# Four 1024 KB transfers per batch cut into pieces of 256 KB, and a new order of work on every engine

## The chip, the cores and the metric

The kernel runs on one core of a Trainium2 chip. The metric is the device time of one execution in microseconds; the smaller the better. Before the change the median of three runs is 2786.49 us.

## What is computed

Eight independent batches of 1024 rows by 256 columns (float32) go through two transformer-like layers. In each, an attention part and a feed-forward part are added to the running activations `x`, and each part works on a layer norm of `x`:

```python
x = x + L0_attn(layernorm(x))   # 8 heads, q/k from projections of size 64; softmax over the heads' own axis (axis=1)
x = x + L0_ffn(layernorm(x))    # gate/up/down, width 704, inputs and weights rounded to blockwise FP4
x = x + L1_attn(layernorm(x))   # 16 heads of 16, layer norm of q and k, softmax
x = x + L1_ffn(layernorm(x))    # dense layer + top-2 of 8 experts of rank 16
```

The input is read from the chip's main memory once, the output is written once, 1024 KB per batch each.

## The kernel before

**Stages and rounds.** A batch goes through four stages, called here A0 (first attention), F (feed-forward), A1 (second attention) and M (experts). They are software-pipelined over batches: in round i the engines do A1 and M of batch i-1, F and the heads (layer norm, q, k, v) of batch i, and the layer norm, projections and A0 of batch i+1. A round has two halves, `lanes_x` (A1 of i-1 with F of i) and `lanes_y` (A0 of i+1 with M of i-1 and the heads of i).

**Order.** Each engine executes one fixed list of instructions. The list is woven from lanes (generator functions, one for each piece of a stage). Every step of a lane has a place, a number in the table `PLACES`; `weave` emits the steps of all lanes of an engine in the order of their places. A round is 129.5 places long, its second half starts at 65.5. A place is an order, no time: an engine waits on semaphores in front of a step, and everything behind it in its list waits too. All transfers of the main loop are issued by SyncE (SP), so its list is one queue: steps that wait hold up all that follow.

**Buffers.** `x[0]` and `x[1]` (1024 KB each in SBUF) hold the running activations of even and odd batches. A batch has to leave its buffer when its heads are done, since batch b+2 is loaded into it while batch b still goes through A1 and M. So four transfers of 1024 KB go with each batch:

- the store (`heads_store`, first step; line 2301): `x[b % 2]` to a scratch tensor `between[b % 2]`, after POOL has added `bproj` to all eight tiles (line 2045, semaphore `xb1_in`);
- the load (`heads_store`, second step; `load_x`, line 2170): input of batch b+2 into the same buffer, after a wait for the store to land;
- the way back (`moe_in`, line 2281): `between` to `x2_` in the region `ub`, after the output of the batch before has left `x2_`;
- the output (`moe_out`, line 2291): `x2_` to `out[b]`.

**Names used below.** `projections(b)` issues the fills (line 2185): copies SBUF to SBUF of 128 KB that bring q and k of A0 to the partitions where TensorE reads them; its steps are pair 1 (0, 1), pair 2 (2, 3) and pair 3 (4, 5), the even step of 8 transfers, the odd one of 4. The scores of A0 step 32 and later (line 624, `pS<-ua`) need pair 2. `heads(b)` stages the q and k of A1: `put` (line 2309) writes 512 KB for a pair of tiles to the scratch `scr`, and six transfers of 64 KB bring the keys back (line 2364); both need POOL's subtraction of line 2079. `ln0(b)` issues the two transposing transfers of A0's normalised input (line 2189), `ffn(b)` those of F's hidden tiles t = 0 to 7 (line 2210). `ln0_values(b)` are the 192 matmuls `pR<-mv,xT`, of which the last 144 read the second half of `ln0`'s transposes. `heads_norm(b)` on POOL has eight steps for a pair of tiles, of which the last two are the subtractions of line 2079.

In SP's list the stretch that matters reads, with the places of one round: projections step 2 (82.20), store (84.33), load (87.60), put of pair 0 and its keys (88.16), projections step 3 (92.82), put of pair 1 (93.31), projections step 4 (97.36).

Of the kernel before, what the change touches and what calls it, by code (L numbers as in the profile page):

```python
# [2486 lines left out]
```

## Time and profile before

| | |
|---|---|
| median of 3 runs | 2786.49 us (2785.46 to 2790.18) |
| profiled execution, time | 2792.73 us |
| its span | 2790.9 us |
| TensorE (PE) busy | 2545.9 us, 91% of the span |
| VectorE (DVE), ScalarE (ACT), POOL busy | 2067.0, 1979.6 and 1203.5 us |
| mean granted TensorE clock | 0.977 |
| bytes moved | 203.51 MB, mean 73 GB/s |

A row of the timeline gives start, duration, engine, line, operation, destination and source, shape and count; in brackets the idle time ahead of it on its engine and what ended it. "issue" there means that the engine waited for nothing that the profile shows. SPq is SP's queue of instructions that issue transfers: a row's duration is the time in which they were issued, not that of the transfer.

### The profile page before, as it was taken

Reading aid. Unit: us, or ns where it says so; the run is one execution under the profiler, and the core shown is the slowest. Engines: PE = TensorE matmul, PEld = TensorE weight load, DVE = VectorE, ACT = ScalarE, POOL = GpSimd, SP = SyncE. Lnnn points to the kernel's source line nnn. Section 1 sums busy time; section 2 is a strip of 40 time slices with the busy share of each in tenths; the row PEclk is TensorE's granted clock in tenths of the full one; section 3 lists DMA queues with packets and bytes.
Section 4 is the critical chain, followed back from the end, with each engine's and each line's share of the span. In section 5 each row is a group of like instructions: output and inputs, shape, how many; then the busy total and the mean of one; then the engine's idle time right before and its main releaser. Section 6 shows DMA issues by size and latency. Waiting matters only on the chain.

```text
span 2790.9 us, 115256 instructions
## 1 busy us (share of the span) xinstructions
PE 2545.9 (91%) x50178; PEld 1408.6 (50%) x50178; DVE 2067.0 (74%) x4266; ACT 1979.6 (71%) x3763; POOL 1203.5 (43%) x1677
## 2 busy tenths in 40 slices
PE   4875797999999989999999999999999999999797
PEld 3533564445644466445654466445663457444333
DVE  7888876867887579866878588876888678875533
ACT  3651366886778867887778867787768877787784
POOL 4662266216642268225653167323762257421210
PEclk9997999999999999999999999999999999999899
DMA  4312333325423252324434253322533253232310
GB/s 122 75 32 41 70 82 96 49 47 99 104 68 76 51 119 66 79 52 84 107 80 65 46 109 79 85 59 52 121 93 54 47 98 93 70 57 48 93 32 17
DMA packets 468766, 203.51 MB, mean 73 GB/s; under 512 B 281020, under 2 KB 458244, under 8 KB 468236
## 3 DMA queue, kind: packets, MB, share of 16 engines
q1 hardware_dynamic: 466268, 194.07, 33.0%
q8 instruction: 413, 6.77, 1.0%
q10 hardware_dynamic: 1968, 1.72, 0.2%
q14 instruction: 117, 0.96, 0.1%
HBM read 46.48 MB, written 32.51 MB: 28 GB/s over the span
## 4 chain that ended last, share of the span: by engine, by line
PE 48%; DVE 19%; issue 8%; ACT 8%; DMA 8%; SPq 5%; POOL 4%; DVEq 0%; POOLq 0%; ACTq 0%
PE pR L624 19%; PE pV L864 11%; PE pS L823 7%; PE pS L624 7%; DVE nmaxa L1434 6%; ACT ub L1140 5%; PE pV L729 3%; SPq L2185 2%; PE pR L634 2%; DMA scr<-ub 2%; DMA xT<-xhb 2%; DMA xT<-ua 1%; DMA ua<-EA 1%; SPq L2389 1%; DMA ua<-ua 1%
## 5 line engine op out<-in xcount | busy, mean ns | idle before, releaser
L1140 ACT ACTIVATE ub<-pS 128x512 f32<-128x512 f32 x2048 | 1049.8, 610 | 168.5 <-PE pS L823 164.9
L1434 DVE TENSOR_REDUCE nmaxa<-pS 128x1 f32<-128x1024 f32 x512 | 621.4, 1215 | 168.8 <-PE pS L624 167.0
L1100 ACT ACTIVATE ua<-pS,nmaxa 128x1024 f32<-128x1024 f32 x384 | 427.6, 1114 | 286.9 <-DVE nmaxa L1434 283.3
L624 PE MATMUL pS<-ua 128*32 128x512 f16 x8192 | 550.4, 387 | 69.3 <-ACT ua L1100 41.3
L864 PE MATMUL pV<-ub,vaug 128*17 128x512 f32 x4096 | 537.0, 598 | 1.0 <-DVE ub L1599 0.7
L1943 POOL TENSOR_TENSOR ua<-ua,rz 128x256 f32<-128x256 f32 x512 | 327.1, 648 | 318.5 <-DVE rz L1443 306.1
L823 PE MATMUL pS<-ub 50*128 50x512 f16 x1920 | 342.5, 385 | 9.0 <-ACT ub L1140 1.6
L624 PEld LDWEIGHTS pS<-ua 128*32 128x32 f16 x8192 | 215.4, 98 | 232.7 <-ACT ua L1100 72.2
L624 PE MATMUL pR<-wgu,xT 128*32 128x352 f16 x6144 | 283.9, 317 | 33.6 <-DVE x L1331 14.1
L729 PE MATMUL pV<-ua 128*32 128x128 f32 x6144 | 246.9, 280 | 27.5 <-POOL ua L1943 16.6
L823 PEld LDWEIGHTS pS<-ub 50*128 50x128 f16 x1920 | 91.9, 93 | 351.6 <-ACT ub L1140 305.0
L624 PEld LDWEIGHTS pR<-wgu,xT 128*32 128x32 f16 x6144 | 160.3, 97 | 181.4 <-issue 113.8
L729 PEld LDWEIGHTS pV<-ua 128*32 128x32 f32 x6144 | 170.1, 112 | 105.7 <-POOL ua L1943 33.4
L1100 ACT ACTIVATE EA<-pS,nmaxa 128x1024 f32<-128x1024 f32 x128 | 142.6, 1114 | 84.9 <-DVE nmaxa L1434 84.8
L1991 POOL TENSOR_TENSOR EA<-ua,EA 128x704 f16<-128x704 f32 x28 | 45.6, 1629 | 363.3 <-DVE EA L1548 363.3
L1991 POOL TENSOR_TENSOR ua<-ua 128x704 f16<-128x704 f32 x28 | 42.9, 1532 | 265.4 <-DVE ua L1548 265.4
L624 PE MATMUL pR<-wqkv,xT 128*32 128x512 f16 (+1 forms) x3072 | 142.9, 326 | 1.0 <-issue 0.6
L624 PE MATMUL pR<-wd,ua 128*32 128x256 f16 x4032 | 135.9, 274 | 6.5 <-DMA ua<-EA 6.3
L624 PEld LDWEIGHTS pR<-wd,ua 128*32 128x32 f16 x4032 | 102.4, 97 | 71.0 <-issue 69.6
L864 PEld LDWEIGHTS pV<-ub,vaug 128*17 128x17 f32 x4096 | 87.3, 96 | 95.2 <-issue 76.0
L1048 ACT ACTIVATE ua<-pR 128x512 f16<-128x512 f32 x128 | 76.5, 605 | 68.5 <-PE pR L624 66.6
L1317 DVE SCALAR_TENSOR_TENSOR ua<-pR,ua 128x512 f16<-128x512 f32 x128 | 86.7, 683 | 50.6 <-ACT ua L1048 49.4
(260 smaller groups left out, 3998.0 us busy)
## 6 DMA issues: line engine op xcount, KB each, us to landing
ua<-ua SPq DMA_DIRECT2D x384, 128.0 KB, 2.7
ub<-scr SPq DMA_DIRECT2D x264, 64.0 KB, 2.8
scr<-ub SPq DMA_DIRECT2D x30, 512.0 KB, 3.8
x<-in_L_attn_x SPq DMA_DIRECT2D x8, 1024.0 KB, 6.2
between<-x SPq DMA_DIRECT2D x7, 1024.0 KB, 5.5
ub<-between SPq DMA_DIRECT2D x7, 1024.0 KB, 5.5
out<-ub SPq DMA_DIRECT2D x7, 1024.0 KB, 4.8
ub<-scr SPq DMA_DIRECT2D x192, 32.0 KB, 1.9
```

The lines of the kernel that those rows point to most:

```text
L624: i = e.matmul(dst[j:j + 32], w[:, j:j + 32], m, start=start, stop=stop)
L634: return e.matmul(dst, src, ident[0:n, 0:n], is_transpose=True)
L729: i = e.matmul(pV[32 * jl:32 * jl + 32, 128 * jg:128 * jg + 128], vs[n % 4][:, j, :], EA[n % 4][:, 128 * j:128 * j + 128], start=(c == 0 a ...
L823: e.matmul(pS[:, 512 * hl:512 * hl + 512], kk_[row:row + 50, o, 128 * c:128 * c + 128], q[row:row + 50, o, 512 * qh:512 * qh + 512]).then_ ...
L864: i = e.matmul(pV[32 * hl:32 * hl + 17, :], vaug[:, c, 4 * hg + hl, :], EB[(4 * n + hl) % 8], start=(c == 0), stop=(c == 7))
L1048: e.activation(dst, view(bank(u)), ACT.Copy, scale=scale).then_inc(r_mid[u.bank], 1)
L1100: e.activation(EA[n % 4], pS[:, 1024 * (n % 2):1024 * (n % 2) + 1024], ACT.Exp, bias=nmaxa[:, n % 32:n % 32 + 1], accum_out=zz[:, n % 8:n ...
L1140: e.activation(EB[(4 * n + hl) % 8], pS[:, 512 * hl:512 * hl + 512], ACT.Exp).then_inc(e1_in, 1)
L1317: e.scalar_tensor_tensor(dst, view(bank(u)), scale, hi, ALU.mult, ALU.subtract).then_inc(r_free[u.bank], 1)
L1434: e.tensor_reduce(nmaxa[:, n % 32:n % 32 + 1], pS[:, 1024 * (n % 2):1024 * (n % 2) + 1024], AXX, ALU.max, negate=True).then_inc(max0_in, 1)
L1943: e.tensor_tensor(vs[m % 4], vv[:, :, 32 * c:32 * c + 32], rz[:, c:c + 1].unsqueeze(2).to_broadcast([128, 8, 32]), ALU.mult).then_inc(vs_i ...
L1991: e.tensor_tensor(pair[:, 1, 0:FI], h_[b > 0][t % 2][:, 0:FI], pair[:, 0, 0:FI], ALU.subtract).then_inc(hlh_in, 1)
```

## The change

Each of the four transfers is divided into four of 256 KB (two tiles of 128 rows each), and each piece is a step of its own with a place of its own. The semaphores' targets rise from 16 to 64 per batch. The first two inputs, loaded ahead of the main loop, stay whole. A store piece waits for the two tiles that it carries, an output piece for its two tiles; the first load piece waits for all four stores, and the first piece of the way back for all four outputs of the batch before and all four stores. The transfers of this kind grow from 29 issues (7 stores, 6 loads, 7 back, 9 outputs) to 112 (28, 24, 28 and 32).

```diff
@timed("SP")
def moe_in(b):
     if b:
-        e.wait_ge(out_in, 16 * b)
-    e.wait_ge(stored[b % 2], 16 * (b // 2 + 1))
-    e.dma_start(x2_[b], tiles_of(between[b % 2])).then_inc(back_in, 16)
+        e.wait_ge(out_in, 64 * b)
+    e.wait_ge(stored[b % 2], 64 * (b // 2 + 1))
+    for tp in range(4):
+        if tp:
+            yield
+        at = slice(2 * tp, 2 * tp + 2)
+        e.dma_start(x2_[b][:, at, :], tiles_of(between[b % 2])[:, at, :]).then_inc(back_in, 16)
...
def moe_out(b, hf=None):
-    ts = tiles_in(hf)
-    yield
-    for t in ts[-3:]:
-        u = ring["base", b, t]
-        e.wait_ge(r_free[u.bank], u.n)
-    at = slice(ts[0], ts[-1] + 1)
-    e.dma_start(tiles_of(out[b])[:, at, :], x2_[b][:, at, :]).then_inc(out_in, 16)
+    for tp in pairs_in(hf):
+        yield
+        for t in (2 * tp, 2 * tp + 1):
+            u = ring["base", b, t]
+            e.wait_ge(r_free[u.bank], u.n)
+        at = slice(2 * tp, 2 * tp + 2)
+        e.dma_start(tiles_of(out[b])[:, at, :], x2_[b][:, at, :]).then_inc(out_in, 16)
...
def heads_store(b):
-    yield
-    e.wait_ge(xb1_in, 8 * b + 8)
-    if b > 1:
-        e.wait_ge(back_in, 16 * (b - 1))
-    e.dma_start(tiles_of(between[b % 2]), x[b % 2][:, :, :]).then_inc(stored[b % 2], 16)
-    if b + 2 < NB:
-        yield
-        e.wait_ge(stored[b % 2], 16 * (b // 2 + 1))
-        load_x(b + 2)
+    for tp in range(4):
+        yield
+        e.wait_ge(xb1_in, 8 * b + 2 * tp + 2)
+        if b > 1:
+            e.wait_ge(back_in, 64 * (b - 1))
+        at = slice(2 * tp, 2 * tp + 2)
+        e.dma_start(tiles_of(between[b % 2])[:, at, :], x[b % 2][:, at, :]).then_inc(stored[b % 2], 16)
+    for tp in range(4) if b + 2 < NB else ():
+        yield
+        e.wait_ge(stored[b % 2], 64 * (b // 2 + 1))
+        at = slice(2 * tp, 2 * tp + 2)
+        e.dma_start(x[b % 2][:, at, :], tiles_of(a["L0_attn_x"][b + 2])[:, at, :]).then_inc(x_in[b % 2], 16)
```

All of `PLACES` is replaced, for all five engines. The places of SP that the text speaks of:

```diff
-    ('SP', 'ln0'): (30.779, 35.832, 59.701),
+    ('SP', 'ln0'): (28.916, 43.914, 63.197),
-    ('SP', 'projections'): (8.841, 11.123, 16.701, 27.32, 31.859, 36.451),
+    ('SP', 'projections'): (10.165, 12.142, 19.215, 26.848, 31.374, 40.978),
-    ('SP', 'ffn'): (11.941, 14.831, 25.011, 25.011, 37.416, 47.163, 47.163, 53.092),
+    ('SP', 'ffn'): (9.523, 13.091, 23.114, 27.274, 41.345, 41.345, 41.345, 59.21),
-    ('SP', 'heads_store'): (18.828, 22.101),
+    ('SP', 'heads_store'): (19.959, 19.959, 19.959, 20.644, 20.644, 20.644, 20.644, 20.644),
-    ('SP', 'heads'): (22.656, 22.656, 22.656, 27.812, 33.091, 42.003, 42.003, 46.9, 46.9, 51.877),
+    ('SP', 'heads'): (29.195, 29.195, 30.489, 32.416, 39.437, 56.949, 56.949, 56.949, 56.949, 56.949),
-    ('SP', 'moe_in'): (10.817,),
+    ('SP', 'moe_in'): (18.178, 18.178, 18.178, 18.178),
-    ('SP', 'moe_out'): (60.957,),
+    ('SP', 'moe_out'): (60.227, 63.571, 64.012, 64.012),
```

In SP's list the same stretch now reads: projections step 2, four stores, four loads, projections step 3, put of pair 0, its keys, projections step 4, put of pair 1. The way back moves from ahead of F's transpose 0 to behind the second of `ffn_in`; `ln0`'s second transpose moves from ahead of F's transpose 4 to behind its transpose 6. On TensorE the last 144 matmuls of `ln0_values` move from place 40.12 to 51.72, which is just ahead of the down projection of F's tile 6. On POOL the last two of the eight additions of line 2045 move from ahead of the last two steps of the first pair's `heads_norm` to behind them and behind two of A0's multiplications (line 1943). The other steps change places by a few steps at most in the rounds of the steady part; the first two and the last two rounds are reordered more.

## Rows read from the trace of the kernel before

**Rows 1.** The page, busy time, share and instructions of TensorE.
```profile
PE 2545.9 (91%) x50178; PEld 1408.6 (50%) x50178; DVE 2067.0 (74%) x4266; ACT 1979.6 (71%) x3763; POOL 1203.5 (43%) x1677
```
**Rows 2.** Windows, busy time by engine, clock, DMA share, GB/s: the steady part.
```profile
400.00:2560.00 2160.00, 2067.86 (x41020) 1140.13 (x41012) 1640.61 (x3329) 1663.48 (x3155) 976.35 (x1374) 0.99 0.36 76
```
**Rows 3.** Timeline of SP's queue around the load at 1349 us.
```profile
1343.04 0.57 SPq L2301 DMA_DIRECT2D between<-x  x1
1348.97 0.40 SPq L2170 DMA_DIRECT2D x<-in_L_attn_x  x1
1349.59 0.52 SPq L2309 DMA_DIRECT2D scr<-ub  x1
1357.70 3.69 SPq L2364 DMA_DIRECT2D ub<-scr  x6
1361.49 3.35 SPq L2185 DMA_DIRECT2D ua<-ua  x4
```
**Rows 4.** Timeline of TensorE, same stretch: the rows with idle time ahead.
```profile
1357.92 0.30 PE L729 MATMUL pV<-ua 128*32 128x128 f32 x2 [1.80 <-issue]
...
1366.79 1.05 PE L624 MATMUL pS<-ua 128*32 128x512 f16 x16 [1.95 <-DMA ua<-ua]
```
**Rows 5.** Timeline of SP's queue: the first, second and last load.
```profile
415.42 0.41 SPq L2170 DMA_DIRECT2D x<-in_L_attn_x  x1
...
706.60 0.40 SPq L2170 DMA_DIRECT2D x<-in_L_attn_x  x1
...
1993.65 0.39 SPq L2170 DMA_DIRECT2D x<-in_L_attn_x  x1
```
**Rows 6.** Timeline of TensorE: the gaps after the second and the last load.
```profile
715.53 1.47 PE L624 MATMUL pS<-ua 128*32 128x512 f16 x11 [2.44 <-issue]
...
2001.70 0.52 PE L729 MATMUL pV<-ua 128*32 128x128 f32 x10 [1.82 <-issue]
```
**Rows 7.** Windows: a long train of fills and transposes; the load with its put.
```profile
1600.00:1610.00 10.00, 9.73 (x72) 2.33 (x73) 1.27 (x4) 9.96 (x21) 2.78 (x4) 1.00 0.98 196
...
1352.00:1356.00 4.00, 4.00 (x139) 2.93 (x127) 4.00 (x6) 3.06 (x6) 1.99 (x5) 1.00 1.04 316
```
**Rows 8.** DMA queues, and issues by size with us to landing.
```profile
q8 instruction: 413, 6.77, 1.0%
...
ua<-ua SPq DMA_DIRECT2D x384, 128.0 KB, 2.7
...
between<-x SPq DMA_DIRECT2D x7, 1024.0 KB, 5.5
```
**Rows 9.** Waits of SP's queue over the whole run: us, times, longest.
```profile
SPq L2170 <- DMA between<-x: 29.6, 6, 5.8
SPq L2281 <- DMA out<-ub: 26.1, 6, 4.8
```
**Rows 10.** Timeline of POOL ahead of the load at 1349 us.
```profile
1340.85 1.42 POOL L2045 TENSOR_TENSOR x<-x,bproj 128x256 f32<-128x256 f32 x2
...
1348.36 1.16 POOL L2079 TENSOR_TENSOR ub<-ub 128x512 f16<-128x512 f32 x1 [0.17 <-ACT ub L1236]
1349.47 1.19 POOL L1943 TENSOR_TENSOR ua<-ua,rz 128x256 f32<-128x256 f32 x2
```
**Rows 11.** Timeline of SP's queue: the way back, and F's first transpose.
```profile
1445.31 0.38 SPq L2281 DMA_DIRECT2D ub<-between  x1
1464.24 1.46 SPq L2210 DMA_TRANSPOSE ua<-ua  x1
```
**Rows 12.** Timeline of SP's queue: `ln0`'s second transpose, F's transpose 6.
```profile
1533.19 1.79 SPq L2189 DMA_TRANSPOSE xT<-ua  x1
...
1571.78 1.43 SPq L2210 DMA_TRANSPOSE ua<-ua  x1
```
**Rows 13.** Timeline of TensorE: the 144 matmuls, the down projection of tile 6.
```profile
1544.46 4.10 PE L624 MATMUL pR<-mv,xT 128*32 128x256 f16 x144
...
1576.71 1.17 PE L624 MATMUL pR<-wd,ua 128*32 128x256 f16 x36
```

More of the change, by code:

```diff
@@ L157 @@
-    ('DVE', 'moe_gate', 7, 1): (31.197, 31.197, 31.197, 31.197, 32.777, 34.316, 34.316, 40.262, 47.559, 48.26, 66.705, 81.132),
-    ('DVE', 'moe_M'): (14.938, 14.938, 14.938, 14.938),
-    ('DVE', 'moe_M', 7, 0): (16.488, 16.488),
-    ('DVE', 'moe_M', 7, 1): (29.279, 29.279),
[59 rows of a table added]
+    ('ACT', 'projections'): (1.965, 4.721, 8.841, 10.36, 16.964, 19.781, 23.066, 26.115, 30.992, 35.622, 38.52, 41.861),
+    ('ACT', 'prep'): (4.721, 12.046, 12.046, 13.975, 18.263, 23.312, 27.447, 34.31, 35.166, 40.136, 44.542, 48.032, 52.415, 56.904, 56.904, 56.904,
+        66.267),
@@ new lines @@
+    ('ACT', 'prep_heads'): (-13.045,),
+    ('ACT', 'ffn'): (1.443, 3.726, 6.678, 10.041, 15.368, 15.548, 20.651, 24.248, 28.979, 30.016, 34.743, 36.879, 40.767, 43.239, 47.551, 50.053),
+    ('ACT', 'heads'): (5.224, 5.224, 9.893, 9.893),
+    ('ACT', 'heads_norm'): (16.297, 25.003, 34.096, 42.306),
+    ('ACT', 'heads_values'): (14.572, 17.406, 19.936, 25.48, 32.317, 33.775, 40, 46.406),
+    ('ACT', 'heads_T'): (23.153, 32.63, 40.857, 50.704),
+    ('ACT', 'moe_rt'): (18.144, 21.502, 25.506, 28.59),
@@ new lines @@
+    ('ACT', 'moe_gate'): (12.961, 14.627, 14.627, 14.627, 28.649, 36.914, 36.914),
+    ('ACT', 'moe_gate', 6): (30.088, 39.285, 42.229),
+    ('ACT', 'moe_gate', 7, 0): (25.755, 35.439),
+    ('ACT', 'moe_gate', 7, 1): (17.116, 40.477),
+    ('ACT', 'heads_end'): (-3.706, -3.706, -3.706, -3.706),
+    ('ACT', 'heads_norm_end'): (15.44, 15.44, 15.44, 15.44, 18.334, 18.334, 53.296, 53.296),
+    ('ACT', 'moe_end'): (14.565, 14.565, 14.565, 14.565),
+    ('ACT', 'moe_end', 7, 0): (),
[10 rows of a table added]
+    ('DVE', 'projections'): (2.59, 5.595, 9.432, 11.922, 17.7, 20.798, 24.928, 27.817, 32.25, 36.449, 39.576, 42.71),
@@ new lines @@
+    ('DVE', 'ffn'): (2.348, 6.127, 6.127, 8.053, 8.053, 8.926, 8.926, 8.926, 8.926, 8.926, 8.926, 10.414, 10.414, 10.71, 10.71, 12.296, 12.296,
[4 rows of a table added]
+    ('DVE', 'heads'): (6.77, 8.553, 10.923, 12.654),
+    ('DVE', 'heads_bias'): (14.721, 16.43, 17.769, 21.56, 31.969, 34.163, 39.301, 42.826),
+    ('DVE', 'heads_bias', 7): (1.843, 1.843, 4.285, 4.285, 4.499, 4.499, 4.499, 4.499),
+    ('DVE', 'heads_norm'): (17.112, 26.467, 35.652, 44.345),
[9 rows of a table added]
+    ('DVE', 'moe_gate'): (19.02, 22.082, 25.458, 28.215, 28.215, 30.36, 30.385, 32.315, 33.774, 37.589, 37.589, 40.867, 45.269, 48.092, 50.717,
+        55.357, 55.357, 59.417, 61.157),
@@ L161 @@
+    ('DVE', 'moe_gate', 7, 0): (25.137, 25.137, 32.427, 42.546, 44.266, 44.42, 44.42, 44.42, 50.3, 52.005, 55.929, 93.893),
+    ('DVE', 'moe_gate', 7, 1): (46.914, 46.914, 46.914, 46.914, 50.638, 57.793, 57.793, 57.793, 104.714, 104.714, 104.714, 104.714),
+    ('DVE', 'moe_M'): (17.388, 17.388, 17.388, 17.388),
+    ('DVE', 'moe_M', 7, 0): (15.215, 15.215),
+    ('DVE', 'moe_M', 7, 1): (46.702, 46.702),
     ('DVE', 'moe_M', 0): (),
@@ L192 @@
-    ('POOL', 'attn1'): (14.943, 27.26, 32.551, 48.47, 57.253, 57.99, 58.1, 64.088),
-    ('POOL', 'attn1', 7): (15.526, 23.606, 27.006, 36.497),
-    ('POOL', 'moe_rstd'): (10.362,),
-    ('POOL', 'moe_low'): (16.422, 16.422, 17.241, 17.241),
+    ('DVE', 'heads_end'): (-3.185, -0.308, -0.308, -0.308, -0.308, -0.308, -0.308, -0.308, -0.308, -0.308, -0.308, -0.308),
+    ('DVE', 'heads_norm_end'): (4.493, 4.493, 10.613, 10.613, 16.668),
+    ('DVE', 'heads_by_end'): (7.524, 7.543, 22.187, 22.187),
@@ new lines @@
+    ('DVE', 'heads_low_end'): (11.968, 11.968, 23.42, 34.801),
+    ('DVE', 'outputs_end'): (59.278, 75.931),
+    ('POOL', 'spread', '0'): (21.711,),
+    ('POOL', 'spread', 'H'): (-4.74,),
+    ('POOL', 'spread', '0', 1): (8.068,),
+    ('POOL', 'spread', 'H', 7): (-2.807,),
[6 rows of a table added]
+    ('POOL', 'prep'): (67.797,),
+    ('POOL', 'prep_weights'): (1.042, 1.042, 1.042, 1.042, 1.042, 1.042, 4.406, 6.261, 6.261, 6.261, 6.261, 6.261, 9.975, 12.233, 12.233, 12.233,
+        12.233, 17.347, 17.347, 17.347, 17.347, 19.551, 24.391, 24.391, 24.391, 24.391, 24.391, 26.239, 26.239, 28.684, 29.579, 31.093, 31.093,
+        31.093, 32.704, 32.704, 32.704, 35.886, 40.575, 40.575, 40.575, 40.575, 40.575, 41.602, 41.602, 43.461, 43.461, 48.931, 48.931, 48.931,
+        50.014, 53.048, 53.048, 53.048, 53.941, 56.474),
@@ new lines @@
+    ('POOL', 'ffn_in'): (-19.751, -10.38, -9.767, -4.07, 6.621, 16.93),
+    ('POOL', 'ffn_in', 7): (-19.751, -10.38, -9.767, -4.07, 6.621, 16.93),
+    ('POOL', 'ffn'): (4.723, 7.882, 12.103, 19.336, 24.305, 34.13, 43.175, 49.738, 57.172),
+    ('POOL', 'heads'): (-1.832, -1.832, -1.83, 4.695, 4.695, 6.595, 6.595, 9.022, 9.648, 9.648, 12.637, 12.637, 12.637, 17.043, 24.955, 24.955),
+    ('POOL', 'heads_norm'): (17.929, 17.929, 17.929, 19.144, 19.144, 19.144, 23.901, 23.901, 25.325, 25.325, 26.753, 29.917, 29.917, 29.917, 34.424,
[4 rows of a table added]
@@ L196 @@
+    ('POOL', 'moe_rstd'): (11.995,),
+    ('POOL', 'moe_low'): (16.247, 16.247, 16.873, 16.873),
     ('POOL', 'moe_low', 6): (),
@@ L198 @@
     ('POOL', 'moe_low', 7, 1): (),
-    ('POOL', 'moe'): (31.353, 31.353, 33.75, 33.75, 38.001, 42.485, 42.485, 42.485),
-    ('POOL', 'moe', 7, 0): (41.043, 41.043, 41.68, 41.68),
-    ('POOL', 'moe', 7, 1): (32.519, 32.519, 32.519, 37.643),
-    ('POOL', 'heads_end'): (3.692, 16.825, 16.825, 16.825, 16.825, 42.702, 42.702, 42.702, 42.702, 42.702, 42.702, 42.702, 42.702),
-    ('SP', 'ln0'): (30.779, 35.832, 59.701),
-    ('SP', 'ln0', 1): (13.629, 15.256, 31.869),
-    ('SP', 'projections'): (8.841, 11.123, 16.701, 27.32, 31.859, 36.451),
@@ L206 @@
[L206 to L213 removed]
+    ('POOL', 'moe'): (30.426, 30.426, 33.583, 33.583, 39.249, 39.387, 41.218, 41.218),
@@ new lines @@
+    ('POOL', 'moe', 7, 0): (55.235, 55.235, 55.235, 55.235),
+    ('POOL', 'moe', 7, 1): (38.73, 38.73, 38.73, 38.73),
+    ('POOL', 'heads_end'): (12.913, 30.526, 30.526, 30.526, 31.045, 38.442, 38.442, 38.442, 38.442, 38.442, 38.442, 38.442, 38.442),
+    ('SP', 'ln0'): (28.916, 43.914, 63.197),
+    ('SP', 'ln0', 1): (9.854, 14.247, 32.407),
+    ('SP', 'projections'): (10.165, 12.142, 19.215, 26.848, 31.374, 40.978),
+    ('SP', 'prep'): (-0.018, -0.018, 11.162, 11.162, 11.162, 16.031, 20.669, 20.669, 22.563, 22.961, 33.275, 37.153, 37.153, 37.153, 50.064, 50.064,
+        50.064),
@@ L222 @@
-    ('SP', 'moe_M', 7, 0): (9.854,),
+    ('SP', 'moe_A'): (66.338, 67.737),
+    ('SP', 'moe_A', 6): (66.338, 67.737),
+    ('SP', 'moe_A', 7): (38.678,),
+    ('SP', 'moe_M'): (14.962, 18.375),
+    ('SP', 'moe_M', 7, 0): (10.764,),
     ('SP', 'moe_M', 7, 1): (),
-    ('SP', 'moe_out'): (60.957,),
-    ('SP', 'moe_out', 7, 0): (51.869,),
-    ('SP', 'moe_out', 7, 1): (69.363,),
-    ('SP', 'heads_end'): (1.747, 17.264, 17.264, 23.024, 34.694, 34.694, 34.694),
+    ('SP', 'moe_out'): (60.227, 63.571, 64.012, 64.012),
@@ L228 @@
+    ('SP', 'moe_out', 7, 0): (48.315, 48.359),
+    ('SP', 'moe_out', 7, 1): (61.036, 61.552),
+    ('SP', 'heads_end'): (4.807, 16.812, 16.812, 16.812, 16.812, 16.812, 16.812),
 }
```

89 lines of the change are left out of this document (21 added, 68 removed), and 175 rows, old and new, of the table PLACES.

## The prediction

> **What bounds the kernel now.** I read the page first: TensorE is busy for 91% of the span [rows 1]. Then the windows, to see where the other 9% lie. Between 400 and 2560 us, about the steady rounds, TensorE is busy for 2067.9 of 2160 us [rows 2], so only 92 us are idle there and everything else of the idle time is in the start and the end, which the divided transfers hardly touch. A change of transfers can therefore give back some part of 92 us and no more, unless it adds waits. Next I looked in TensorE's timeline for gaps over 1 us in that part and what ended them, and found that the largest sort stands right behind the transfer that is to be divided.
>
> In SP's queue the store is issued at 1343.04; the load, which waits for it to land, at 1348.97; the put of 512 KB 0.6 us behind; the put has landed when the keys are issued at 1357.70, and only then do the four fills of projections step 3 follow, from 1361.49 [rows 3]. TensorE stands still twice: 1.80 us until 1357.92, for "issue", and 1.95 us until 1366.79, for those fills [rows 4]. The first gap ends 8.95 us behind the load and within 0.3 us of the put's landing. This repeats: the loads at 706.60 and 1993.65 [rows 5] have gaps of 2.44 and 1.82 us that end 8.9 and 8.1 us behind them [rows 6]. Of the six loads the last five have one each, together 11.95 us (2.44, 3.35, 1.80, 2.54, 1.82); the first, at 415.42, has none, and the seventh store, behind which there is no load, has none either.
>
> My reading of the gap: while 1.5 MB issued within 1.1 us stand in the transfer engines, the instructions themselves, which come over a queue of their own (413 packets of 16 KB) [rows 8], come late, and TensorE runs out of them about 6 to 7 us after the load. Two rows say what matters is how much stands ahead and not that the engines are busy: in 1600 to 1610 a train of fills and transposes keeps them at a share of 0.98 and TensorE has no such gap, and in 1352 to 1356, behind the load, they are no busier (1.04) [rows 7], but there the whole train was issued at once, while SP issues the fills one by one, every 0.65 us or more.
>
> The Trainium skill (Runtime: NRT & Kernel Launch, section Instruction fetch mechanics) has each engine's instructions refilled in blocks of 16 KiB over a DMA queue; the trace agrees, 6.77 MB in 413 packets. But its DMA: Bandwidth & Descriptors (Queues, rings and completion order) lets an engine go round its queues after each packet of at most 64 descriptors; by that rule bytes in SP's queue would hold the refill only for a packet, and the gaps would stay whatever the division. That is the second rival below.
>
> **The change, part by part.**
>
> *Issues.* 83 more transfers. A row of a load is 0.40 us, of a store 0.57 [rows 3], so 83 x 0.40 to 0.57 = 33 to 47 us more on SP over the run, some 5 us per round. They lie where SP waits anyway: for the landing of the store, 29.6 us in six waits, or for the output, 26.1 us in six [rows 9]. The way back today waits some 4.4 us and is issued at 1445.31, but F's transpose behind it is issued only at 1464.24 when POOL is ready [rows 11]; moving the wait away gives nothing, and four issues further back cost nothing. Without that cover each piece would cost its 0.4 us on the path.
>
> *A piece's landing* is not in the trace. It lies between 2.7 us (128 KB) and 5.5 us (1024 KB) [rows 8]; I take 3.2, nearer the small one.
>
> *Store, load, fills.* The first three stores go as soon as projections step 2 is issued, at 1343, for the first six additions are long done. The fourth needs POOL's last two additions, which move behind the subtraction that ends at 1349.5 and two multiplications of 1.19 us: 1349.5 + 1.2 + 1.42 for the additions = 1352.1 [rows 10]. It lands at 1355.5 or so (0.2 to issue); four loads until 1357.2; four fills of projections step 3 at the pace of 3.35 us until 1360.6. The train loads plus fills is 1.5 MB; at the rate of before, 1.5 MB in 8.1 us, it is through by 1363.6. Before, the fills had landed at 1366.8. The scores asked for them at 1364.84 (1366.79 less 1.95), or at 1363.0 without the gap ahead. So the wait shrinks from 1.95 to about 0.5 us. Three rounds have it (1.62, 1.95, 1.25, sum 4.8, after the loads at 706.6, 1349.0 and 1993.7): I take -3.5, bounds 0 and -4.8.
>
> *The gap.* The load starts 6.5 us later and is issued over 1.7 us, the fills over 3.4 and the put behind them, at 1360.7. With 0.185 MB draining in a us (1.5 MB in 8.1 us) 0.7 MB stand there when the last load is issued, 0.55 MB after the fills, 1.05 MB with the put: 5.7 us at most, against 8 before. TensorE began to stand still 5.7 to 7.1 us after a load. So the gaps mostly go: of 12 us I take -9, bounds 0 and -12 on this reading.
>
> *Put and keys late.* The put of pair 0 goes some 11 us later. Behind it in SP's queue are its keys and projections step 4, which serves scores 16 steps on, 40 us away at 2.5 us a place (324.2 us from load to load over 129.5 places); the keys are for A1, 70 us away. Hidden.
>
> *`ln0`'s second transpose* goes from 1533.19 to behind F's transpose 6, 1571.78 [rows 12]: issued at 1573.2, landed 4.7 us later, at 1577.9. The 144 matmuls (4.10 us) that read it move to just ahead of the down projection that ran at 1576.71 [rows 13]. TensorE gets there 4.1 us earlier, at 1572.6, but the hidden tiles of F come up to 4.1 us earlier too, so transpose 6 may go at 1567.7 and the other land at 1573.8: a wait of 1.2 us, or 5.3 if nothing upstream moves; below, nothing, if it all keeps ahead. Six rounds: 0 to 32 us; nearest is the case in which upstream moves, and part of what is waited there was waited for transpose 6 before. I take +0.4 a round, +2.
>
> *Outputs* in pieces, the last behind the last tile pair: the end gains about 0.3 us (256 KB against 512 KB). *All other places*: steps move by a few; no row prices that. I allow 6 us either way, one wait of 1 us (as long as the fill waits above) opened or closed in each of six rounds.
>
> The Trainium skill (DMA: Bandwidth & Descriptors, Rules for kernel authors) asks for 1 MiB or more per transfer, which speaks against the division; its table gives 6.15 us for 1 MB and 0.95 us for 64 KB. The trace moves 1.5 MB in 8.1 us whichever sizes are in the train, and no run here shows 256 KB. It is the last rival.
>
> **Sum**, against the profiled execution's 2792.7 us: -9 - 3.5 + 2 - 0.3 = -10.8. TensorE that starts sooner meets the next wait sooner, so I let nine tenths through: -10. That execution is 6.2 us above the median of the runs; taken from the median: 2786.5 - 10 = **2776.5**.
>
> **Rivals.**
> 1. *Forecast* (0.53): gaps and fill waits mostly go; 2765 to 2781.
> 2. *No change* (0.22): the refill is held by something that the division doesn't alter, or the time won is waited for elsewhere. For it: the gap-free first load shows that the train isn't enough by itself, and TensorE is 96% busy, with a chain of scores, maximum and exponential that has its own pace. Against: five gaps that all end with the train. The fills alone give -3.5, `ln0` +2: 2785, within 2781 to 2792.
> 3. *`ln0`'s transpose is late* (0.13): upstream moves only by a third, so 3.5 us are waited in six rounds, +21, less the 12.8 that is won: 2794.7. It decides (slower by 0.2%) from 3.1 us a round. For it: VectorE and POOL between a gate matmul and transpose 6 have work of their own, which a sooner TensorE doesn't shorten. Against: 5.3 us takes that none of the chain moves, and it starts from TensorE's matmuls, which do move.
> 4. *The longer train starves TensorE more* (0.08), slower: the refill comes only when the queue runs dry. Then loads, fills and put are one train of 2 MB, 10.8 us in place of 8.1, so 2.7 us more in each of the last five rounds: +13.5 - 3.5 + 2, with 2798.5. It decides from whether the gap's end follows the put's landing. Against: the full train of 1600 to 1610 without a gap.
> 5. *Pieces cost each their own time* (0.04): four landings of 3.2 us in a row, 12.8 in place of 5.5, 7 us later for the fills, waited for 1.5 us more a round in six: 2795.
>
> **Range and chances.** Cases 1 and 2 hold 0.75; the range takes them in and reaches to the end of case 3: 2765 to 2795; the forecast's own is 2765 to 2781. A difference of 0.2% (5.6 us) is about what this measurement can tell from none. Faster by more: 0.55 (case 1 and a rest of 2), same 0.24, slower 0.21.
>
> **What the profile after would show.** Right: no "issue" gap over 1 us within 10 us of a load; the wait of `pS<-ua` for `ua<-ua` there under 0.7 us; the store's wait ahead of the load under 4 us and the load some 6 us later against the put's subtraction; TensorE's idle time between 400 and 2560 near 82 us. Wrong: gaps that still end with the put's landing (case 4); a wait for `xT<-ua` ahead of `pR<-mv,xT` (case 3); the same idle time under other names (case 2). A steady part that is as forecast with another start or end would say that the places, not the pieces, made the difference.

## The result and the profile after

| | before | after |
|---|---|---|
| median of the runs, us | 2787.43 (2785.46 to 2790.18) | 2766.26 (2763.59 to 2770.72) |
| profiled execution: span, us | 2790.9 | 2765.6 |
| granted clock of TensorE, mean | 0.977 | 0.980 |

The ratio is 0.9916, with a 95% interval of 0.9897 to 0.9935: the changed kernel is faster by 21 us, or 0.84%. The direction and the range were right. The forecast of 10 us less was not; the time won is twice that.

The page of the changed kernel, busy time of each engine, with the same 50178 matmuls as before [rows 1]:

```profile
span 2765.6 us, 115376 instructions
PE 2538.1 (92%) x50178; PEld 1402.2 (51%) x50178; DVE 2060.3 (74%) x4266; ACT 1976.2 (71%) x3763; POOL 1186.6 (43%) x1677
```

The span is 25.3 us shorter. Of this 7.8 us are busy time (2545.9 to 2538.1) for the same matmuls, at a mean clock of 0.980 in place of 0.977, and 17.5 us are idle time (245.0 to 227.5). The forecast counted idle time alone. That is the first thing to see.

The windows of the changed kernel for its steady part (columns as in [rows 2]):

```profile
400.00:2540.00 2140.00, 2062.21 (x41066) 1132.40 (x41058) 1633.63 (x3330) 1663.61 (x3161) 959.18 (x1374) 0.99 0.36 77
```

TensorE is idle there for 77.8 us where it was for 92.1; about 82 had been forecast.

**Where in the run.** The first gate and up matmul (`pR<-wgu,xT`) of a batch is a marker that both traces have. Measured from one to the next, the rounds took 321.2, 323.7, 319.9, 324.1, 319.7 and 320.0 us before, and 315.5, 314.3, 319.0, 318.4, 317.0 and 319.6 after: 5.7, 9.4, 0.9, 5.7, 2.7 and 0.4 us less. The marker that the first of these rounds starts from, that of batch 1, stands at 477.51 and at 477.45, so nothing was won ahead of it. The round with 0.4 us is the one that holds no load and had no gap. The time comes from the five rounds that had the gap behind a load, 24.4 us together. The windows over exactly these five rounds, before and after (columns as in [rows 2]):

```profile
477.51:2086.10 1608.59, 1547.11 (x31320) 867.62 (x31321) 1233.80 (x2526) 1232.61 (x2337) 741.78 (x1041) 0.99 0.37 78
477.45:2061.62 1584.17, 1538.69 (x31320) 859.93 (x31321) 1225.56 (x2526) 1230.31 (x2337) 731.12 (x1041) 1.00 0.37 79
```

For the same 31320 matmuls TensorE is idle for 61.5 us before and for 45.5 after, 16.0 less, and busy for 8.4 us less. The 24.4 us are these two.

**SP's queue.** The timeline of SP's queue in the changed kernel, the stretch of [rows 3]:

```profile
1322.43 6.21 SPq L2196 DMA_DIRECT2D ua<-ua  x8
1328.73 9.02 SPq L2318 DMA_DIRECT2D between<-x  x4
1341.02 3.45 SPq L2323 DMA_DIRECT2D x<-in_L_attn_x  x4
1344.56 2.88 SPq L2196 DMA_DIRECT2D ua<-ua  x4
1347.54 1.46 SPq L2327 DMA_DIRECT2D scr<-ub  x1
1352.21 2.68 SPq L2382 DMA_DIRECT2D ub<-scr  x6
```

The four pieces of the store, the four of the load, the four fills and then the put follow each other as the diff has them. The row of the store is 9.02 us long, since its fourth piece waits for POOL's additions. In POOL's timeline of the changed kernel, beside [rows 10]:

```profile
1333.69 1.16 POOL L2090 TENSOR_TENSOR ub<-ub 128x512 f16<-128x512 f32 x1 [0.16 <-ACT ub L1247]
1334.81 1.18 POOL L1954 TENSOR_TENSOR ua<-ua,rz 128x256 f32<-128x256 f32 x2
1335.95 1.42 POOL L2056 TENSOR_TENSOR x<-x,bproj 128x256 f32<-128x256 f32 x2
```

The subtraction ends at 1334.85, the additions at 1337.37, and the load starts at 1341.02, 6.2 us behind the subtraction. The forecast had 2.6 us for the additions and 6.0 for the load. The waits of SP's queue over the run:

```profile
SPq L2318 <- POOL x L2056: 39.9, 8, 7.6
...
SPq L2323 <- DMA between<-x: 16.7, 6, 4.1
```

The store's landing is waited for 2.8 us at a time (16.7 in six) where it was 4.9 (29.6 in six, [rows 9]). The price is the new wait above it, 39.9 us in eight, for the additions.

**TensorE.** No gap for "issue" of over 0.6 us stands within 10 us of a load any more; before there were five, of 1.80 to 3.35 us [rows 4, 6]. One of 1.58 us is left in the steady part; it ends at 792.98, 5 us behind the start of four pieces of the output. (In e11, the same kernel on another chip, it isn't there.) The wait for the fills did not shrink. TensorE's timeline of the changed kernel, the matmuls that answer to the second of [rows 4]:

```profile
720.09 1.05 PE L635 MATMUL pS<-ua 128*32 128x512 f16 x16 [1.55 <-DMA ua<-ua]
...
1350.88 1.58 PE L635 MATMUL pS<-ua 128*32 128x512 f16 x16 [2.67 <-DMA ua<-ua]
...
1988.74 1.05 PE L635 MATMUL pS<-ua 128*32 128x512 f16 x16 [1.87 <-DMA ua<-ua]
```

The three rounds that had it have it still: 6.1 us together, against 4.8. The forecast had named a wait under 0.7 us as a sign of being right; this sign did not come.

**What a gap costs behind itself.** The windows of the kernel before, 10 us each, around the loads at 706.6, 1028.4 and 1349.0 (the eighth column, behind POOL, is the granted clock):

```profile
715.00:725.00 10.00, 8.07 (x163) 5.22 (x163) 6.44 (x33) 3.62 (x6) 4.62 (x10) 0.83 0.35 75
1028.00:1038.00 10.00, 6.02 (x188) 4.61 (x180) 5.55 (x13) 6.46 (x13) 5.32 (x13) 0.91 0.53 160
1038.00:1048.00 10.00, 10.00 (x182) 5.83 (x178) 6.38 (x36) 4.09 (x9) 2.88 (x7) 0.74 0.36 76
1349.00:1359.00 10.00, 8.20 (x239) 5.84 (x231) 7.19 (x20) 7.70 (x18) 6.15 (x16) 1.00 0.55 163
```

And of the changed kernel: the first four are the same stretches, counted from the marker of the round; the last is the one stretch near a load in which the clock falls, behind its wait of 2.67 us for the fills:

```profile
715.00:725.00 10.00, 8.45 (x216) 6.06 (x210) 7.75 (x44) 5.79 (x12) 6.37 (x12) 1.00 0.62 159
1022.00:1032.00 10.00, 10.00 (x270) 6.44 (x266) 9.84 (x38) 7.85 (x18) 6.57 (x18) 1.00 0.59 177
1032.00:1042.00 10.00, 9.71 (x248) 7.01 (x242) 9.00 (x25) 7.13 (x13) 7.91 (x13) 1.00 0.32 87
1334.00:1344.00 10.00, 9.89 (x296) 6.52 (x286) 9.17 (x23) 8.11 (x19) 7.31 (x17) 1.00 0.27 80
1351.00:1361.00 10.00, 10.00 (x192) 6.69 (x189) 8.19 (x18) 7.79 (x14) 5.74 (x7) 0.83 0.12 33
```

TensorE does 163 matmuls in 715 to 725 before and 216 after. (The two lists are not in the same order, so the matmuls of two windows are alike and not the same.) The rows of the clock have two levels, 1.2 and 2.4 GHz: 1.00 is 2.4 GHz throughout, and 0.74 means that about half of the window ran at 1.2. In 1038 to 1048 TensorE is shown busy for all of 10.00 us and still does 182 matmuls, where it does 248 in 1032 to 1042 after: this loss is not idle time and no list of gaps shows it. Behind the five gaps, what is missing from a clock of 1.00 comes to 8.6 us before; after, in the same stretches, to 1.7 us, in 1351 to 1361.

That is not the whole of the clock, though. In the same five rounds it also falls where no such gap stands: before, at 1442 and 1487 (3.4 us missing), and after, at 1426 and 1744 (5.1 us missing). There too it follows idle time of TensorE, under other names: 3.22 us of wait for `xT<-ua` and 1.51 for `ua<-EA` before, 2.54 and 3.07 us for `xT<-ua` after. Over the five rounds 11.9 us are missing before and 6.8 after, so the net is 5.1 us. In e11, which is the changed kernel once more, 3.4 are missing; so much differs from one execution to the next.

### The profile page after: what moved, and what is told of

The parts are those of the page before. It is cut to its first block, busy times and chain, and to the rows that moved or that the text cites. A ratio compares the mean times of both kernels' runs of the same rounds, so it can differ in the third digit from the quotient of the medians.

```text
span 2765.6 us, 115376 instructions
## 1 busy us (share of the span) xinstructions
PE 2538.1 (92%) x50178; PEld 1402.2 (51%) x50178; DVE 2060.3 (74%) x4266; ACT 1976.2 (71%) x3763; POOL 1186.6 (43%) x1677
## 4 chain that ended last, share of the span: by engine, by line
PE 50%; DVE 20%; ACT 9%; DMA 7%; issue 6%; POOL 5%; SPq 4%; DVEq 0%; POOLq 0%; ACTq 0%
PE pR L635 19%; PE pV L875 12%; PE pS L834 8%; DVE nmaxa L1445 7%; ACT ub L1151 6%; PE pS L635 6%; PE pV L740 3%; PE pR L645 2%; DMA xT<-ua 2%; SPq L2196 2%; DMA xT<-xhb 1%; SPq L2407 1%; POOL ua L1954 1%; DMA ua<-EA 1%; DVE ua L1328 1%
## 5 line engine op out<-in xcount | busy, mean ns | idle before, releaser
L635 PE MATMUL pS<-ua 128*32 128x512 f16 x8192 | 539.9, 384 | 49.6 <-ACT ua L1111 24.1
L1954 POOL TENSOR_TENSOR ua<-ua,rz 128x256 f32<-128x256 f32 x512 | 333.1, 663 | 266.5 <-DVE rz L1454 256.4
L834 PE MATMUL pS<-ub 50*128 50x512 f16 x1920 | 336.9, 384 | 8.8 <-ACT ub L1151 1.6
L635 PEld LDWEIGHTS pS<-ua 128*32 128x32 f16 x8192 | 208.6, 97 | 210.1 <-ACT ua L1111 47.0
L740 PE MATMUL pV<-ua 128*32 128x128 f32 x6144 | 240.5, 277 | 27.4 <-POOL ua L1954 24.8
L1509 DVE SCALAR_TENSOR_TENSOR ua<-ua,pR 128x352 f32<-128x352 f32 x112 | 58.0, 517 | 77.5 <-ACT ua L1122 76.4
```

What stands on the lines that cost most here:

```text
L635: i = e.matmul(dst[j:j + 32], w[:, j:j + 32], m, start=start, stop=stop)
L740: i = e.matmul(pV[32 * jl:32 * jl + 32, 128 * jg:128 * jg + 128], vs[n % 4][:, j, :], EA[n % 4][:, 128 * j:128 * j + 128], start=(c == 0 a ...
L834: e.matmul(pS[:, 512 * hl:512 * hl + 512], kk_[row:row + 50, o, 128 * c:128 * c + 128], q[row:row + 50, o, 512 * qh:512 * qh + 512]).then_ ...
L1509: e.scalar_tensor_tensor(ht[hv][:, FH:2 * FH], ht[hv][:, 0:FH], 1.0, bank(g)[:, 0:FH], ALU.add, ALU.mult).then_inc(r_free[g.bank], 1)
L1954: e.tensor_tensor(vs[m % 4], vv[:, :, 32 * c:32 * c + 32], rz[:, c:c + 1].unsqueeze(2).to_broadcast([128, 8, 32]), ALU.mult).then_inc(vs_i ...
```

## The experiments

Twelve kernels ran, on three chips (e1 to e4, e5 to e8, e9 to e12), each beside the kernel before on the same chip. That took 2794.2, 2796.07 and 2795.51 us there, so ratios are what compares.

| | edit | median, us | ratio [95%] | gaps behind load or burst, us | waits for the fills, us |
|---|---|---|---|---|---|
| e1 | old, put and keys of pair 0 behind the fills | 2774.47 | 0.9935 [0.9915, 0.9954] | 0.65, 1.01, 0.90, 1.01 | none |
| e2 | old places, all in pieces | 2788.10 | 0.9981 [0.9960, 1.0002] | 1.10, 1.61, 0.74 | 16.6 |
| e3 | old, load at place 40 | 2772.80 | 0.9930 [0.9907, 0.9953] | 0.94, 0.96 | none |
| e4 | new places, all whole | 2788.34 | 0.9985 [0.9967, 1.0003] | none | 22.5 |
| e5 | changed, load pieces at 41.5 | 2761.41 | 0.9866 [0.9837, 0.9895] | none | none |
| e6 | new places, only the store in pieces | 2769.78 | 0.9906 [0.9876, 0.9935] | none | 5.1 |
| e7 | changed, 1 MB more ahead of pair 2's put | 2766.61 | 0.9889 [0.9850, 0.9927] | 0.68 | 7.9 |
| e8 | changed, 2 MB more there | 2774.98 | 0.9919 [0.9891, 0.9947] | 1.55, 0.70, 0.74, 0.77 | 7.1 |
| e9 | e1 and e3 together | 2770.23 | 0.9924 [0.9892, 0.9956] | 1.25, 0.77 | none |
| e10 | new places, all whole, load at 41.5 | 2766.38 | 0.9911 [0.9877, 0.9945] | 1.55, 1.38 | none |
| e11 | changed kernel again | 2770.30 | 0.9922 [0.9896, 0.9949] | none | 6.7 |
| e12 | e5 again | 2761.48 | 0.9888 [0.9850, 0.9926] | none | none |

Gaps are those of 0.6 us and more for "issue" within 15 us of the load or burst; the waits for the fills are those of 0.8 us and more of `pS<-ua` for `ua<-ua` behind the store and load, summed over the rounds.

### e1: only the put and the keys moved

```diff
-    ('SP', 'heads'): (22.656, 22.656, 22.656, 27.812, ...
+    ('SP', 'heads'): (27.4, 27.4, 27.4, 27.812, ...
```

> The kernel before with whole transfers of 1024 KB; only the put of pair 0 and its keys go behind projections step 3, so that four fills, issued one by one, stand between load and put. Theory Q (the queue: a load and a put issued within 1.1 us starve TensorE, which costs the gap, a lower granted clock behind it, and the late fills): the five gaps named issue go or shrink under 1 us, 2766 to 2773 us. Theory P (the gain is in the new places of the other lanes): 2783 to 2788 us, gaps or not. Theory D (the division itself is what keeps instructions coming): gaps of 1.8 us and more stay, 2782 to 2790 us.

One lane's three steps, in whole transfers, give 0.9935. The timeline of SP's queue in e1, the stretch of [rows 3]:

```profile
1345.21 0.40 SPq L2170 DMA_DIRECT2D x<-in_L_attn_x  x1
1351.03 2.59 SPq L2185 DMA_DIRECT2D ua<-ua  x4
1353.72 0.55 SPq L2309 DMA_DIRECT2D scr<-ub  x1
```

Before, the put stood between load and fills, and the keys behind it waited for its landing, so the fills went 12.5 us behind the load; here they go 5.8 behind it, and TensorE waits for none of them. The gaps shrink to 1.01 us or less (theory Q had them under 1) and the clock is 1.00 in every window there. So the put behind the load is what made most of both losses, and its move gives most of the gain with nothing divided.

The same trace shows something else. A gap of 2.51 us ends at 485.03, where the kernel before has none; 7 us ahead of its end, at 478.00, SP issued the way back, another 1024 KB and nothing with it. The gap is not the load's own, then: another 1 MB that falls badly makes one too. And the granted clock is 0.83 in that trace's window of 480 to 490.

### e2: only the pieces, at the old places

All four transfers divided as in the diff of the change; every piece at the old place of its transfer.

```diff
-    ('SP', 'heads_store'): (18.828, 22.101),
+    ('SP', 'heads_store'): (18.828, 18.828, 18.828, 18.828, 22.101, 22.101, 22.101, 22.101),
```

> All four transfers in pieces of 256 KB, with the places of the kernel before (each piece at the place of the whole). Theory Q: the load's pieces are issued over 1.7 us with the put right behind, so 1.5 MB still come within 2.5 us: at least three gaps over 1 us stay, 2778 to 2788 us. Theory D: no gap, 2764 to 2772 us. Theory P: 2783 to 2790 us.

0.9981: the pieces alone give next to nothing. (Theory Q had at least three gaps over 1 us; there are two.) TensorE's timeline of e2, the matmuls of [rows 4]:

```profile
1355.28 0.30 PE L729 MATMUL pV<-ua 128*32 128x128 f32 x2 [1.61 <-issue]
...
1364.41 1.05 PE L624 MATMUL pS<-ua 128*32 128x512 f16 x16 [2.21 <-DMA ua<-ua]
```

and of SP's queue:

```profile
1346.60 2.10 SPq L2312 DMA_DIRECT2D x<-in_L_attn_x  x4
1348.81 0.42 SPq L2316 DMA_DIRECT2D scr<-ub  x1
...
1359.36 3.14 SPq L2185 DMA_DIRECT2D ua<-ua  x4
```

The gaps shrink in number and size, from 11.95 us to 3.5, and the waits for the fills take their place: 3.41, 3.91, 2.21, 3.99 and 3.05 us, 16.6 in place of 4.8, with clocks down to 0.66 behind them. The keys still wait for the put, and the fills stand behind the keys.

### e3: only the load moved away

```diff
-    ('SP', 'heads_store'): (18.828, 22.101),
+    ('SP', 'heads_store'): (18.828, 40.0),
```

> The kernel before with whole transfers; only the load moves, from right behind the store to behind the keys of pair 1 (place 40 of 64), where nothing else is due. Theory Q: no issue gap behind the load, SP doesn't wait for the store, put and fills are earlier by some 5 us: 2762 to 2769 us. Theory D: a whole load of 1 MB still starves TensorE, at its new place: gaps over 1 us there, 2775 us or more. Theory P: 2783 to 2788 us.

0.993. The load goes at place 40, some 50 us later in its round (the first one 14), and in five rounds right ahead of another put of 512 KB: 1.5 MB issued within 1.3 us in four of them and within 2.4 in the fifth. Yet only two of the six have a gap, of 0.94 and 0.96 us, and no fill of projections step 3 stands behind them. The same bytes cost less at another place. Here too a gap of 2.26 us ends 7 us behind the first way back, at 489.16.

### e4: new places, the transfers whole

```diff
-    ('SP', 'heads_store'): (19.959, 19.959, 19.959, 20.644, 20.644, 20.644, 20.644, 20.644),
+    ('SP', 'heads_store'): (20.644, 20.644),
```

with the way back at 18.178 and the output at 64.012.

> The new places of all lanes, but the four transfers whole, each at the place of its last piece of its kind (the load at its own). Theory Q: load and put are apart as in the changed kernel, no gap over 1 us: 2764 to 2774 us. Theory D: gaps of 1.8 us and more are back, 2778 to 2790 us. Theory P: 2764 to 2770 us.

0.9985: the new places alone give next to nothing either. No theory had this: Q was right on the gaps and wrong on the time, D the other way round. SP's queue in e4:

```profile
1348.19 0.40 SPq L2312 DMA_DIRECT2D between<-x  x1
1353.67 0.40 SPq L2181 DMA_DIRECT2D x<-in_L_attn_x  x1
1354.17 2.81 SPq L2196 DMA_DIRECT2D ua<-ua  x4
1357.08 0.59 SPq L2320 DMA_DIRECT2D scr<-ub  x1
```

and TensorE behind it:

```profile
1363.56 1.90 PE L635 MATMUL pS<-ua 128*32 128x512 f16 x16 [4.56 <-DMA ua<-ua]
```

No gap is left, with the four fills between load and put. But the whole store waits for all eight additions, the load for the store's landing, and the fills for both, in one queue: 5.70, 4.46, 4.56, 4.28 and 3.46 us are waited for them. So the change works in two halves that need each other: the places take the gaps away and would put the fills late, and the divided store brings these back in time. One thing is not separated: at the new places TensorE also does other work just there. It starts 41 to 49 matmuls and weight loads per us in the 6 us behind the loads of e4, where the kernel before mostly starts 58 to 63, so the fills between load and put may not be all that took the gaps away.

### e5: the changed kernel with its load away

```diff
-    ('SP', 'heads_store'): (19.959, 19.959, 19.959, 20.644, 20.644, 20.644, 20.644, 20.644),
+    ('SP', 'heads_store'): (19.959, 19.959, 19.959, 20.644, 41.5, 41.5, 41.5, 41.5),
```

> The changed kernel with its four load pieces moved from right behind the stores to behind projections step 5 (place 41.5). Theory Q (the queue around store, load, put and fills): SP no longer waits there for the stores, the fills of projections step 3 no longer stand behind the load, so the three waits of 1.6 to 2.7 us for them go: 0.2 to 0.4% faster than the changed kernel, ratio to the kernel before 0.987 to 0.990. Theory P (the other lanes' places are what counts): as the changed kernel, 0.991 to 0.993.

0.9866, with neither gap nor wait for the fills, and just below the range of theory Q.

### e6: which of the four divisions counts

New places; the store in pieces, the load, the way back and the output whole.

```diff
+    ('SP', 'heads_store'): (19.959, 19.959, 19.959, 20.644, 20.644),
+    ('SP', 'moe_in'): (18.178,),
+    ('SP', 'moe_out'): (64.012,),
```

> New places of all lanes, the store in four pieces, load, way back and output whole. Theory S (of the division only the store's matters, because three of its pieces leave ahead of POOL's last additions and the last lands sooner): ratio 0.990 to 0.994, waits for the fills of 1.5 to 3 us. Theory L (the load's pieces matter, because the fills get in between them): waits for the fills of 3.5 to 5.7 us as with all transfers whole, ratio 0.997 to 1.000.

0.9906, the changed kernel's own 0.9916 within the interval, and against 0.9985 with the store whole. Of the four divisions the store's is the one that shows.

### e7 and e8: the bytes alone

In the changed kernel a step of SP at place 41.5 copies 1 MB (e7), or twice 1 MB (e8), into a spare tensor in six rounds; pair 2's put of 512 KB follows at once. The copies are added work.

```diff
+                for k in range(2):
+                    e.dma_start(tiles_of(spare[k]), src).then_inc(spare_in, 16)
```

> The changed kernel with one more transfer of 1024 KB (SBUF to a spare tensor, same row size as the store) in each of six rounds at place 41.5, where the queue is quiet. Theory B (bytes issued at once, counted from the issue, starve TensorE when they take longer than 6 to 7 us to drain): 5.5 us alone in the queue, no issue gap over 1 us behind it, 0 to 5 us more than the changed kernel (ratio 0.991 to 0.994). Theory N (any large whole transfer does it): a gap of 1.8 us and more behind each.

> The same with two transfers of 1024 KB issued back to back. Theory B: they drain in about 10.8 us, so behind each pair TensorE stands still for 3.5 to 5 us named issue, ending 10 to 12 us behind the first, and its granted clock falls behind the gap: six times 5 to 8 us, ratio 1.000 to 1.009. Theory R (instructions get their turn among the data after each packet): no gap, ratio 0.991 to 0.995.

e7 has 1.5 MB issued within 1.3 to 1.5 us in four of its six rounds (2.3 and 3.4 us in the other two), where the kernel before had 1.1 us, and no gap over 0.68 us. e8 has 2.5 MB there, within 2 to 4.2 us, and its largest gap is 1.55 us. SP's queue and TensorE in e8:

```profile
1068.92 3.46 SPq L2324 DMA_DIRECT2D spare<-wgu  x2
1072.42 0.69 SPq L2345 DMA_DIRECT2D scr<-ub  x1
```

```profile
1080.63 0.40 PE L640 MATMUL pS<-ua 128*32 128x512 f16 x4 [1.55 <-issue]
```

I had expected gaps of 3.5 to 5 us in all six. That bytes issued at once are enough to make the gap is refuted.

What tells these rounds apart is seen in the queue that carries instructions, q8, and in TensorE's pace. The DMA view of the kernel before, 1349 to 1355 and then 1355 to 1357, the load at 1348.97 ahead of both (columns: packets, MB, share of the 16 engines):

```profile
q1 hardware_dynamic: 1404, 1.24, 69.4%
...
q8 instruction: 1, 0.02, 2.7%
```

In the first six microseconds the data queue moves 1404 packets and q8 none; q8's next packet comes in the two after. Behind the last five loads q8's packets stand at about -0.5, +6.5 and +10 us from the load (all within 1 us), so one interval of 6.2 to 7.4 us lies over the load. e1 is the test of this: at the same places, with the same whole load and the put moved away, that interval is 4.6 to 5.6 us in the same five rounds. In the round of 1349 q8's packet is there within the first six microseconds, 1345 to 1351 in e1:

```profile
q1 hardware_dynamic: 1040, 1.05, 55.6%
q8 instruction: 1, 0.02, 1.1%
```

TensorE's pace is nearly the same in both: in the 6 us behind the load it starts 58 to 63 matmuls and weight loads per us before (47 in one round) and 58 to 59 in e1 (50 in one round). The gap stands in the long interval. The gap of e1 at 485.03 fits too: q8's packet comes 1.0 us behind the first way back in the kernel before and 4.6 us behind it in e1 and e3, the two that have a gap there.

Behind the first load at 415.42, the one without a gap, the interval is as long, 7.4 us, but TensorE starts only 48 per us. At place 41.5 its pace is 50 to 52, and the interval over the burst is 6 to 8.4 us in e7 and 6.5 to 8.9 in e8: longer than the old ones in part, with less missing. In e3 too the two rounds with a gap are those with an interval over 8 us (8.0 and 8.4; the other three with a put have 5.8 to 6.8). So the gap is what the delayed interval is longer than TensorE can go on at its pace in that stretch. That fits the other traces in the main, not everywhere: in e2 a gap of 1.10 us stands at an interval of 5.3 us, in e10 one of 1.55 at 7.5. The view doesn't say for which engine a packet of q8 is. So this is a reading of the rows and not shown by a run.

In e8 one packet of q8 comes while its train is still running, in 1393 to 1395:

```profile
q1 hardware_dynamic: 658, 0.67, 101.2%
q8 instruction: 1, 0.02, 2.9%
```

The data queue fills the engines there, 6 us into a train of 2.5 MB, and the refill comes all the same: it does not wait until the queue is dry.

### e9 to e12: what is worth building

e9 has both moves on the old kernel (e1's and e3's), in whole transfers; e10 is e4 with the load at 41.5; e11 and e12 are the changed kernel and e5 again.

> The kernel before with whole transfers and two moves in SP's list: put and keys of pair 0 behind projections step 3, and the load to place 40. Theory Q (the queue around store, load, put and fills is all): neither gaps over 1 us nor waits for the fills, ratio to the kernel before 0.990 to 0.994, no better than either move alone by more than 0.3%. If the other lanes' new places are worth something of their own, this stays behind the changed kernel with the late load (0.9866) by 0.3% or more.

> The new places with all transfers whole (0.9985 as it was), now with the load at place 41.5 instead of ahead of the fills. If the division was needed only because store and load stand ahead of the fills: the waits for the fills fall from 3.5 to 5.7 us to under 2 us, ratio 0.987 to 0.992. If division is worth something by itself beyond that: 0.993 or more.

> The changed kernel itself, for a comparison on one chip: ratio 0.990 to 0.993.

> The changed kernel with the load's pieces at place 41.5 once more, beside the changed kernel on one chip: 0.2 to 0.5% faster than it, ratio 0.986 to 0.990.

e9 comes to 0.9924, no better than e1 or e3 alone, as if both moves cured the same thing. Its expectation of no gap over 1 us is missed by one of 1.25. SP's queue in e10 and then in e12:

```profile
1337.57 0.40 SPq L2312 DMA_DIRECT2D between<-x  x1
...
1340.64 3.46 SPq L2196 DMA_DIRECT2D ua<-ua  x4
```

```profile
1338.81 3.82 SPq L2196 DMA_DIRECT2D ua<-ua  x4
...
1379.73 2.17 SPq L2323 DMA_DIRECT2D x<-in_L_attn_x  x4
1381.94 0.47 SPq L2327 DMA_DIRECT2D scr<-ub  x1
```

With the load away even the whole store does no harm to the fills (e10: none waited for, against 22.5 us in e4). e10 keeps two gaps, of 1.55 and 1.38 us, each behind a whole load with a put at its heels (three other loads stand so and have none); e12, whose load is in pieces there, has none, and is 4.9 us (0.18%) faster on the same chip. That fits a small gain from the load's pieces, but the intervals overlap. The best version is the changed kernel with its load at 41.5: 2761.4 and 2761.5 us, the second against 2770.3 for the changed kernel on the same chip, 0.32% less, though the intervals of the two ratios overlap.

## Why the forecast was right in kind and wrong in size

**The step that failed** is the sum, "-9 - 3.5 + 2 - 0.3 = -10.8", of which nine tenths were let through. All its terms are idle time of TensorE; the clock is put at nothing without a reason, and the other lanes' places at 0 with 6 us either way. Over the five rounds the runs showed this in its place:

| term | forecast, us | measured in the five rounds, us |
|---|---|---|
| waits for "issue", the gaps above all | -9 | -10.3 (12.8 to 2.5) |
| waits for the fills | -3.5 | +0.5 (6.1 to 6.6, all of `ua<-ua`; +1.3 in the three rounds that have them behind a load) |
| waits for the transposes `xT<-ua` | +2 | +2.8 (7.2 to 10.0) |
| all other waits of TensorE | 0, 6 either way | -9.0 |
| busy time | none | -8.4, of which 5.1 missing clock |
| outputs, at the end of the run | -0.3 | not in these rounds |
| sum | -10.8 | -24.4 |

**The gaps.** Right as a mechanism, and nearly as a size of idle time: of the 11.95 us in five gaps none is left, and 9 had been counted. e1 shows that the put's distance from the load does it. What the term left out is what an idle stretch costs behind itself. That this is no matter of the new places is seen in e1 and e3, which have the old ones. In the same five rounds e1 has 11.3 us less idle time, 5.1 less missing clock and is 15.1 us shorter than the kernel before; e3 has 12.4 and 8.5 and is 18.2 shorter. So a third to a half again comes on top of the idle time, not as much again. That the clock falls because of the gap is argued from the rows (it falls behind them, most behind the largest, is 1.00 at the same stretches in e1, e3 and e5, and 0.83 where e1 and e3 have new gaps of 2.51 and 2.26 us; and it falls behind waits of other names too: e4, with no gap and 22.5 us of waits for the fills, has 17.1 us missing); no run changed the clock by itself. Of the 8.4 us of busy time 3.3 stay unexplained.

**The other waits.** In the five rounds TensorE's waits for ScalarE went from 19.8 us to 8.8 and those for VectorE from 2.9 to none, while those for POOL rose from 0.8 to 9.2. This looks like a gap's wake and is not: e1, e3 and e9, without the old gaps at the old places, wait 22.2, 21.9 and 22.6 us for ScalarE, and e4, with the new places and no time won, 7.2. It is the new places that trade one sort of wait for another, and the forecast's "no row prices that" left it at nothing.

**"I let nine tenths through"** went the wrong way: what TensorE won in a gap was not, on the whole, waited for later.

**The fills' wait.** Forecast -3.5, measured +1.3. Counted from the marker of the round (1122.40 before, 1107.29 after) TensorE asks for them at 240.9 us (1350.88 less 2.67), where the forecast's 1363.0 is 240.6: right. But they had landed at 243.6 us where I had 1363.6, which is 241.2. The load starts as forecast; its row is 3.45 us long where I had 1.7 from 0.40 us an issue, and this puts the fills 1.8 us later. That is the part of this term that was mis-sized. In e2 the same four issues take 2.10 us; what makes them longer here the trace doesn't name. Without the division of the store the wait is 22.5 us (e4).

**`ln0`'s transpose** (+2, and rival 3). In the round of 1349 us it is issued at 1551.20, right behind F's transpose 6 at 1549.70, and the 144 matmuls at 1554.58 aren't held. Upstream had moved far enough: counted from the marker that transpose is 7 us earlier than before. In the whole steady part I find two waits within its 144 matmuls, 1.01 us at 606.02 and 0.35 at 1235.36. TensorE's waits for transposes did rise (10.2 to 16.0 us from 400 us on), but at other matmuls.

**Way back, outputs, issues.** Hidden, as forecast: the way back goes at 1476.41 in four pieces between F's transposes at 1464.48 and 1480.77, and e6, which has it whole, takes the same time.

**A piece's landing.** The page of the changed kernel has 3.2 us for the store's pieces, as I took it, and 3.9 for the load's:

```profile
between<-x SPq DMA_DIRECT2D x28, 256.0 KB, 3.2
...
x<-in_L_attn_x SPq DMA_DIRECT2D x24, 256.0 KB, 3.9
```

Rival 5 is out: the wait for the store's landing ahead of the load is 2.8 us at a time and not 12.8, and e6, which has only the store in pieces, and the changed kernel take the same time.

**The reading of the gap, and rivals 2 and 4.** "How much stands ahead" was half of it. The refill is late behind 1.5 MB in every round, but a gap of 1.8 us and more stood only where TensorE was using up its instructions fast (behind the old loads) or behind the first way back (e1, e3); e7 and e8 have the late refill and little gap. Rival 4, the refill only when the queue runs dry, falls with e8's packet amid the train. Rival 2 falls with the gaps themselves, and the time won was not waited for elsewhere. The rule beside it, of an engine that goes round its queues packet by packet (the Trainium skill, DMA: Bandwidth & Descriptors, section Queues, rings and completion order), would have q8 wait for one packet; here it is absent for 6 us while q1 moves 1404. What holds it that long is open. A run that changes the size of the packets at the same bytes would have told more; I did not make it.

**The places of the other lanes.** Allowed for with 6 us either way. Whatever they give lies between e9 (old places, 0.9924) and e10 or e12 (new places, 0.9911 and 0.9888) on one chip: 0.1 to 0.4%, with overlapping intervals, so it isn't settled.
